# Expert stage of an audio tower: the first product turned round, its weights held by the array instead of its rows

## The reference, cut to what matters

```python
x_red = x @ w_red;  logits = x_red @ wg_n.T
gates = softmax(logits); scores = max(gates); idx = argmax(gates)
h = x @ W1[idx] + b1[idx]          # 256 -> 512
h = gelu(h, approximate=False)
o = (h @ W2[idx] + b2[idx]) * scores   # 512 -> 256
out = x_before_norm + o
```

## Time and profile before

| | us |
|---|---|
| median of 3 runs | 557.06 (554.93 to 557.14) |
| the profiled execution, its own time | 554.61 |
| its span, first to last instruction | 552.9 |
| TensorE busy in the span | 511.7 (93%) |
| VectorE busy | 454.5 (82%) |

### The profile page before, as it was taken

One profiled execution on the slowest core, in us unless ns is written; L12 is line 12 of the kernel. 1 busy time (PEld: TensorE's weight loads), 2 busy tenths in 40 slices (PEclk: granted clock), 3 DMA queues, 4 the chain that ended last, 5 costly groups with the idle time before them and its releaser, 6 DMA issues. The chain is left out here.

```text
span 552.9 us, 12548 instructions
## 1 busy us (share of the span) xinstructions
PE 511.7 (93%) x3439; PEld 368.3 (67%) x3439; DVE 454.5 (82%) x1180; ACT 231.4 (42%) x447; POOL 193.1 (35%) x283
## 2 busy tenths in 40 slices
PE   5998999999999999999988879999868999999992
PEld 4875667766677766777654657777436777777771
DVE  2878888988889888888898899999858888888881
ACT  0436354664545554545635421222105444444440
POOL 5553323312232213222121212222142656665642
PEclk9999999999999999999998998999989999999997
DMA  5711212122122121221123033443521222222320
GB/s 126 249 40 38 76 40 76 43 71 76 38 76 67 47 76 47 67 76 38 38 54 97 24 99 98 114 107 92 209 96 41 85 73 86 74 81 79 78 56 1
DMA packets 34937, 42.14 MB, mean 76 GB/s; under 512 B 8454, under 2 KB 26103, under 8 KB 34644
## 3 DMA queue, kind: packets, MB, share of 16 engines
q1 hardware_dynamic: 25508, 27.59, 16.5%
q0 software_dynamic: 3744, 9.34, 5.8%
q10 hardware_dynamic: 5648, 4.75, 2.8%
HBM read 32.97 MB, written 9.59 MB: 77 GB/s over the span
## 5 line engine op out<-in xcount | busy, mean ns | idle before, releaser
L533 PE MATMUL banks<-proj,xnT_h 128*128 128x512 f16 x384 | 115.1, 382 | 4.3 <-DVE early L1231 4.2
L514 PE MATMUL banks<-early 128*128 128x256 f16 x768 | 86.8, 273 | 1.1 <-DVE early L1206 1.1
L514 PEld LDWEIGHTS banks<-early 128*128 128x128 f16 x768 | 75.1, 98 | 9.7 <-DVE early L1206 1.4
L533 PE MATMUL banks<-proj,xnT_l 128*128 128x512 f16 x192 | 73.1, 381 | 0.0
L533 PEld LDWEIGHTS banks<-proj,xnT_h 128*128 128x128 f16 x384 | 37.5, 98 | 41.2 <-DVE early L1231 4.9
L1855 POOL DMA_INDIRECT vo<-token_rows,vo x39 | 40.1, 1028 | 54.8 <-DVE proj L1689 35.3
L767 PE MATMUL banks<-w2h,vo 128*128 x312 | 57.5, 273 | 0.2 <-DVE vo L1664 0.2
L748 PE MATMUL banks<-w1h,vo 128*128 x156 | 52.9, 380 | 2.8 <-DVE vo L1657 2.8
L1003 ACT ACTIVATE vo<-banks 128x256 f16<-128x256 f32 x39 | 14.9, 383 | 81.0 <-PE banks L735 81.0
L1793 POOL TENSOR_TENSOR w1l<-stage,w1h 128x512 f32 (+1 forms) x16 | 19.0, 1186 | 84.0 <-ACT w1h L887 84.0
L1860 POOL DMA_INDIRECT out<-proj,vo x39 | 39.8, 1020 | 18.8 <-issue 10.8
(11 more groups left out here) (259 smaller groups left out, 1256.5 us busy)
## 6 DMA issues: line engine op xcount, KB each, us to landing
early<-in_x SPq DMA_DIRECT2D x16, 512.0 KB, 3.3
stage<-in_W SPq DMA_DIRECT2D x32, 256.0 KB, 2.8
early<-lam_by_chunk SPq DMA_DIRECT2D x32, 68.0 KB
token_rows<-rows ACTq DMA_DIRECT2D x16, 129.0 KB, 2.5
early<-lam_by_head SPq DMA_DIRECT2D x16, 128.0 KB, 3.0
rows<-in_b SPq DMA_DIRECT2D x1, 2048.0 KB, 7.1
token_rows<-rows ACTq DMA_DIRECT2D x16, 112.9 KB, 2.0
rows<-in_b SPq DMA_DIRECT2D x1, 1024.0 KB, 9.2
```

The lines of the kernel that those rows point to most:

```text
L514: last = mm(bank(2 + j, D), x_[:, k, at:at + P], w[:, KG * half + k, :], start=(half == 0 and k == 0 and x_ is gT_h and w is wtok_h), stop ...
L533: last = mm(dst, a, c, start=(i == 0), stop=(i == n - 1))
```

## The change

The first product is turned round. The array now holds a 128x128 block of W1, and the 128 rows of the slot stream by, so that the result has units on partitions: 24 products of 128 columns (L782) take the place of 6 of 512, and the gelu's output needs no transposes before `down`. The bias b1 now is one value per partition: it is loaded once as 32 rows of 128, transposed once (L717), kept as `b1_turned`, and given to the gelu as its bias. The gelu becomes four instructions per slot, of 128 columns each, reading PSUM. `xh`, `xl` have two buffers. On TensorE the order is `transpose_rows(i+1)`, `up(i)`, `down(i-1)`. The addresses of a slot's weights are worked out a slot ahead, by groups between products. Two waits of TensorE (on `pre_done` in `up`, on `y_steps` in `down`) are gone.

In routing, the ids are found first, in a pass of their own (39 columns), and the scores later in a second pass (78 columns) after `keep_busy(10)`; VectorE's work on scores moves behind `at_place`, and its last steps (`keep_scores`) behind `norm_rows(1)`. The two operations that prepare the exponent's argument move from VectorE to GpSimd. `keep_busy(9)` is added in the mix stage, after the third tile of pair 1. b1 is no longer spread over partitions by DMA; b2 still is.

```diff
+            pool.wait_ge(s["mx_done"], 1)
+            ptt(lg, rows[:, :, ROWC:ROWT], mx.unsqueeze(2).to_broadcast(T8), ALU.subtract).then_inc(s["lg_steps"], 1)
...
+            ptt(lg, lg, rows[:, :, 1:2].to_broadcast(T8), ALU.mult).then_inc(s["r_args"], 1)
...
             def pair(p, ahead=True):
                 for k in range(4):
                     mix(p, k)
+                    if (p, k) == (1, 2):
+                        keep_busy(9)
...
-            keep_busy(28)
+            keep_busy(30)
+            pe.wait_ge(s["carried_ready"], 1)
+            find(found_ids, 0, 1).then_inc(s["found_ready"], 1)
+            keep_busy(10)
             pe.wait_ge(s["carried_ready"], 3)
+            find(banks[:, 7, 0:2 * SLOTS], 1, 2).then_inc(s["scores_found"], 1)
...
+            def up(i, v, expert, between):
                 pe.wait_ge(s["xdl_done"], i + 1)
-                if i >= 1:
-                    pe.wait_ge(s["pre_done"], i)
-                for c in range(DC):
-                    for x_, w in ((xh, w1h), (xh, w1l), (xl, w1h)):
-                        last = mm(bank(0), x_[:, c, :], w[:, bass.ds(e * DC + c, 1), :].rearrange("p a b -> p (a b)"),
...
                 for f in range(FC):
+                    for c in range(DC):
+                        for part, x_ in ((0, xh), (1, xh), (0, xl)):
+                            last = mm(banks[:, 4 * v + f // 2, f % 2 * P:f % 2 * P + P], expert.to_units[f, c, part],
+                                      x_[:, v, c, :], start=(c == 0 and part == 0 and x_ is xh),
+                                      stop=(c == DC - 1 and x_ is xl))
+                    if f % 2 == 1:
+                        last.then_inc(s["m1_ready"], 1)
+                    between(f)
...
             for i in range(SLOTS):
+                more = i + 1 < SLOTS
+                if more:
                     transpose_rows(i + 1)
+                def within_up(f):
+                    if f == 0 and more:
+                        experts[i + 1] = Expert(i + 1)
+                    if f >= 1:
+                        experts[i].place_rows(*((), (0,), (1,), (2, 3))[f])
+                def within_down(f):
+                    if more:
+                        experts[i + 1].place_units(f)
+                up(i, i % 2, experts[i], within_up)
                 if i >= 1:
+                    down(i - 1, (i - 1) % 2, experts[i - 1], within_down)
...
+            def gelu(i, w, e):
...
+                for f in range(FC):
+                    if f % 2 == 0:
+                        act.wait_ge(s["m1_ready"], 2 * i + f // 2 + 1)
+                    af(gel[:, w, f, :], banks[:, 4 * w + f // 2, f % 2 * P:f % 2 * P + P], ACT.Gelu,
+                       bias=b1_turned[:, bass.ds(e * FC + f, 1)]).then_inc(s["gelu_done"], 1)
```

More of the change, by code:

```diff
@@ L762, in down @@
+            def down(i, w, expert, between):
                 pe.wait_ge(s["g_done"], i + 1)
-                if i >= 2:
-                    pe.wait_ge(s["y_steps"], i - 1)
                 for f in range(FC):
-                    for a, w_ in ((gh, w2h), (gh, w2l), (gl, w2h)):
-                        last = mm(bank(3 + 3 * w, D), a[:, w, f, :], w_[:, bass.ds(e * FC + f, 1), :].rearrange("p a b -> p (a b)"),
-                                  start=(f == 0 and w_ is w2h and a is gh), stop=(f == FC - 1 and a is gl))
+                    for a, part in ((gh, 0), (gh, 1), (gl, 0)):
+                        last = mm(bank(3 + 3 * w, D), a[:, w, f, :], expert.to_rows[f, part],
+                                  start=(f == 0 and part == 0 and a is gh), stop=(f == FC - 1 and a is gl))
+                    between(f)
@@ L1018, in _ @@
             for i in range(SLOTS):
+                e = expert_of(i)
                 if i + 1 < SLOTS:
-                    split_rows(i + 1)
-                if i >= 1:
-                    split_gelu(i - 1, (i - 1) % 2)
-                gelu(i, i % 2)
-            split_gelu(SLOTS - 1, (SLOTS - 1) % 2)
+                    split_rows(i + 1, (i + 1) % 2)
+                gelu(i, i % 2, e)
+                split_gelu(i, i % 2)
         @block.vector
@@ L1562, in _ @@
             tt(oh, repeated(rank_w16[:], T8), wide(mw, T8), ALU.is_equal).then_inc(s["oh_ready"], 1)
-            r.step(tt(lg, raw_lg, wide(mx, T8), ALU.subtract))
-            dve.wait_ge(s["rstd2_ready"], TILES)
-            r.settle()
-            tt(lg, lg, rows[:, :, 1:2].to_broadcast(T8), ALU.mult).then_inc(s["r_args"], 1)
             dve.wait_ge(s["counts"], 1)
@@ L1603, in _ @@
                       slot_twice[:].unsqueeze(1).to_broadcast(TS), ALU.is_equal))
+            r.settle()
+            tt(carried[:, :, 0], in_slot, by_pairs(ids16[:]).unsqueeze(2).to_broadcast(TS),
+               ALU.mult).then_inc(s["carried_ready"], 1)
+            for q in range(4):
+                four = slice(4 * q, 4 * q + 4)
+                TP = [P, 4, P, 2]
+                tt(at_place[:, four], by_pairs(place_of)[:, four].unsqueeze(2).to_broadcast(TP),
+                   place_twice[:].unsqueeze(1).to_broadcast(TP), ALU.is_equal).then_inc(s["places_ready"], 1)
             dve.wait_ge(s["r_exp"], 1)
@@ L1611, in _ @@
             r.step(tt(score, score, valid[:], ALU.mult))
+            dve.wait_ge(s["found_ready"], 1)
+            ts(gather_id, found_ids, float(ID_MIDDLE), None, ALU.add).then_inc(s["route_ready"], 1)
             r.settle()
@@ L1619, in _ @@
                    ALU.mult).then_inc(s["carried_ready"], 1)
-            for q in range(4):
-                four = slice(4 * q, 4 * q + 4)
-                TP = [P, 4, P, 2]
-                tt(at_place[:, four], by_pairs(place_of)[:, four].unsqueeze(2).to_broadcast(TP),
-                   place_twice[:].unsqueeze(1).to_broadcast(TP), ALU.is_equal).then_inc(s["places_ready"], 1)
             S7 = [P, SLOTS, E - 1]
```

186 lines of the change are left out of this document (95 added, 91 removed).

## The result

Compared with the kernel before on the same chip, in turns, the changed kernel took 536.09 us (median of 4: 536.06 to 537.96), the kernel before 556.77; the ratio is 0.9642, 95% interval 0.961 to 0.9674. The forecast was about 536. A ratio is taken over a kernel's executions within 1.5% of its fastest one, a median over all of them. The experiments say what is different there, and what stays open.

What follows compares the result with a forecast made beforehand. TensorE, never resting in the expert stage, bounds the kernel. 554.61 less 19.8 (last `finish` earlier) less 0.7 (mix) gives 534.1; with 2.45 added back, about 536 us. Forecast range 533 to 539.5, wider range 532 to 546.

Steps and rivals of the forecast that it cites:

- The slot: TensorE's expert stage: 24 `up` products 0.056 apart, gelu transposes gone; 3.26 us per slot falls to 2.87.
- The sequencer: TensorE's issue work per slot: sum 2.66 us, or 2.4 with less overlap; under 2.87, so costed at nothing.
- (b): Rival in `up`: narrow products go at weight-load pace, 0.098 each; slot 3.88, time 574 us; chance 0.06.
- (a): Rival: sequencer or ScalarE's biases make the slot 2.95 to 3.2, time 539 to 549; chance 0.22 together with (d).
- (c): Rival not spelled out in the prediction; sign: TensorE issue idle inside `up`; no gain, near 556 upward; chance 0.05.
- ScalarE: Expert stage: four short gelus of about 0.26 each raise its busy time per slot from 1.50 to 1.9 us.
- GpSimd: Expert stage: gather and scatter 1.0 each plus two gaps of 0.31, 2.6 us per slot, under 2.87.
- The mix: Mix stage: nine added products fill a TensorE gap; -0.7 us if the clock stays up, otherwise 0.
- Routing: Ahead of the expert stage: first gather at 403.85 instead of 407.59, first `up` 3.2 us earlier, at 409.55.
- (d): Rival in routing: reordering doesn't bring gathers forward; 3.2 us stays, time 539; chance 0.22 together with (a).
- First slots: Start of expert stage: first `up` 409.55, `up(1)` 411.8 to 413.15; a clock fall costs at most 1.7 us.
- hidden, by 0.7: Chain from `up(i)` through the gelu to `down(i)`: 2.1 us, while TensorE has 2.87 of other work.

Runs made afterwards that it cites:

- e9: Changed kernel with every product's weight address worked out at issue instead of a slot ahead; 574.98 us, 1.0159 of the kernel before.
- e5: Changed kernel as it is, run again beside the kernel before; 536.41 us, ratio 0.964.
- e6: Changed kernel plus filler products in the first slots, 6 behind the scores pass and 7 ahead of the second transpose; 536.5 us, ratio 0.9642.
- e11: Changed kernel as it is, in a later set on another chip; 591.75 us, 1.0486 of the kernel before (565.29).
- e7: Changed kernel with the exponent's two preparing operations back from GpSimd to VectorE, ahead of the scan; 535.89 us, ratio 0.9643.
- four experiments: Changed kernel with addresses at use; also expert 0 always; 8 of 12 `down` products; ids and scores in one pass: 575.97, 565.34, 590.5, 594.99 us.

## Why the prediction was right, and where it was not

Where it was measured it held, point by point:

- **The slot**: 2.87 predicted and 2.87 measured, in 35 of the 38 distances between the first products of `up` (2.99 and 3.60 at the start, 2.65 at the end). The 0.056 of the nearest row carries over from a burst of 8 to 24 in every slot. Rival (b), the pace of weight loads, is out by the rows: loads of 0.098 start 0.056 apart, and some 0.02 apart at 39 columns.
- **The sequencer**: hidden, as costed; rivals (a) and (c) are out, since TensorE has no idle time "issue" from 420 to 520. The terms were a little off: the expert's load takes 0.49 at the median instead of 0.30, the steps 0.07 instead of 0.06. With them my sum per slot is 2.97, more than the slot, or 2.7 by its lower reading; since TensorE had no idle time, the upper one counted too much. The step is right all the same, and e9 shows what is hidden by the order, 0.94 per slot.
- **ScalarE**: 15.47 busy in 20 us is 2.22 per slot against 1.9. The term that was mis-sized is the short gelu, 0.26 estimated, 0.364 by its group. It was cut off too low by drawing a line through 256 and 512 columns of two different functions.
- **GpSimd**: 2.6 predicted. In the groups from 420 to 515 gather and scatter last 1.135 and 1.121 on the mean, where they took 1.02 and 1.03, with 0.61 of gaps 2.87, the slot itself. That looks like a full engine and is not one: each gather starts 0.80 after its `finish`, and a scatter is recorded at 1.32 ahead of the longest distance between two `finish` (3.07) and at 1.02 behind it. When GpSimd does have a backlog, the pair takes 2.78. That is the number to set against the slot, 0.2 more than I gave: it is the next bound that the traces show, 0.1 below the slot.
- **The mix**: -0.7 predicted, -0.81 measured. From the stage's first transpose to its last product it is 83.02 before (306.12 to 389.14) and 82.21 after, 82.19, 82.20 and 82.18 in e5, e6 and e11.
- **Routing**: the first gather was to come 3.74 earlier (407.59 to 403.85). Counted from the reduction it came 3.42 earlier, 17.03 before (390.56 to 407.59) and 13.61 after. The 0.35 for the two operations moved to GpSimd is the part that was wrong: e7 makes it 0. Rival (d) is out.
- **First slots**: from the first gather to the first `up` 5.70 predicted, 6.08 measured. From the first `up` to the first `down` 3.60 predicted, 5.06 measured (409.00 to 414.06). The term that the sum left at nothing is the clock, for which the text allowed up to 1.7: in `up(0)` alone it took 1.17 of the 1.46 (2.45 against e6's 1.28), and e6 with the clock whole has 3.71 in all. I took the fall as a possibility only, although it was plain that TensorE would idle there; the row of the idle time should have decided it.
- **The end**: 109.6 from the first `down` to the last `finish` predicted (413.15 to 522.75), 109.80 measured.

In sum the last `finish` came 18.66 earlier and not 20.5, and the profiled execution ended at 536.06, not 534.1. Of the 18.66, 0.44 arose ahead of the mix, which began at 305.68 and not 306.12. That the median still met 536 is partly chance: the 2.45 between the profiled execution of before and its median does not belong to the kernel, and after has none. Its likely source shows in the traces: the mix begins anywhere from 305.15 to 308.19 in the fourteen traces, whatever the kernel.

**Where it was wrong** is the claim that the wait for the gelu is "hidden, by 0.7". It is hidden as long as completions reach their semaphores at once: in the changed kernel's first trace the chain takes 2.15 (2.1 predicted), and VectorE's low part ends 0.56 ahead of its `down` in most slots. Before, the split ended 1.58 ahead of it. Under the conditions of e11 completions come late, and the kernel goes from 0.964 to 1.049. Every step of the forecast went by durations; none asked what a late hand-over costs each of the two kernels. Why the changed kernel loses 56 us (591.75 against 536) there and the one before 9 was not settled, because no trace of the one before was taken under them. What fits the rows is only argued: 0.56 is less than one late completion (1.69 on the mean), TensorE's slot has become shorter than the chain through ScalarE and VectorE plus one late completion, and each idle time brings its clock down too.

## What to carry to other kernels

A slot is won by the pace of the narrow product in the nearest burst, not by the duration of its weight load; read starts, not durations. When one engine's slot has been cut, look for the next bound where that engine has a backlog, not in the mean of its durations: GpSimd's pair seemed to fill the new slot of 2.87 us, and takes 2.78 when nothing holds it. A gain that rests on hand-overs hidden by less than a microsecond should be measured in more than one set of runs, with the unchanged and the changed kernel in each, before it or any experiment on it is believed: four experiments here were first read without that control, and would have blamed the wrong edits.

## What the hardware showed that I had not expected

- TensorE's completions can reach their semaphores up to 4 us after the product's modelled end, while its own rows go on at full pace and ScalarE's and VectorE's completions are on time; in the expert stage only, and only in those sets of runs in which the kernel before takes 564 to 566 instead of 556 to 557. The cause is open.
- VectorE's half-precision operation on 128x256 takes 0.66 us beside GpSimd's on the same size in single precision, 0.29 without it.
- Indirect gathers and scatters of 128 rows last 1.135 and 1.121 us with the shorter slots, 1.02 and 1.03 before; with a backlog the pair takes 2.78 with its gaps. A mean duration of the scatter can hold waiting.
- A gelu of 128 columns takes 0.364 us, a plain copy of 256 columns 0.383.
- A load of the expert's number into TensorE's register takes 0.30 to 0.57 us in the changed kernel, 0.30 at the median before.
